# A decoder layer in one software pipeline: new instruction orders on all five engines, cross-attention turns issued singly, one-element VectorE copies removed

## The reference, cut to what matters

```python
x = x + attn(layernorm(x))              # 16 heads of 8, rope, causal
x = x + xattn(layernorm(x), ctx)        # 16 heads of 8, 77 context rows
x = x + ffn(layernorm(x))

def ffn(x):
    probs = softmax(x @ router_w)                     # 8 experts
    top1_val, top1_idx = top_1(probs)
    hid = (x @ up_w[e]) * silu(x @ gate_w[e])         # 7 routed experts
    routed = sum over e of (hid @ down_w[e]) * (top1_idx == e)
    shared = ((x @ shared_up) * silu(x @ shared_gate)) @ shared_down
    return 2.0 * top1_val * routed + shared
```

## Time and profile before

| | |
|---|---|
| median of 3 runs | 1080.29 us (1079.55 to 1080.8) |
| profiled execution, its own time | 1076.56 us |
| its span | 1074.7 us |
| TensorE busy, matmuls | 987.1 us (92%) |
| TensorE busy, weight loads | 819.5 us (76%) |
| VectorE busy | 870.5 us (81%) |
| ScalarE busy | 738.3 us (69%) |
| GpSimd busy | 631.6 us (59%) |

### The profile page before, as it was taken

One profiled execution on the slowest core, in us unless ns is written; L12 is line 12 of the kernel. 1 busy time (PEld: TensorE's weight loads), 2 busy tenths in 40 slices (PEclk: granted clock), 3 DMA queues, 4 the chain that ended last, 5 costly groups with the idle time before them and its releaser, 6 DMA issues.

```text
span 1074.7 us, 45099 instructions
## 1 busy us (share of the span) xinstructions
PE 987.1 (92%) x16200; PEld 819.5 (76%) x16201; DVE 870.5 (81%) x2853; ACT 738.3 (69%) x1557; POOL 631.6 (59%) x1488
## 2 busy tenths in 40 slices
PE   1578999999999999999999999999999889999995
PEld 1356777777777777777777777777777889999995
DVE  3367999989999999989999999999996557777774
ACT  0266887888888787888878888887875245555552
POOL 0345667776767767676677767677664224444443
PEclk9999999999999999999999999999999999999998
DMA  5222111000010000000000000100010122222220
GB/s 132 70 71 71 33 29 32 28 28 27 25 32 26 30 25 28 29 25 30 25 29 28 25 30 25 31 26 30 26 28 24 60 66 71 72 68 71 67 67 5
DMA packets 66648, 44.27 MB, mean 41 GB/s; under 512 B 24135, under 2 KB 61451, under 8 KB 66592
## 3 DMA queue, kind: packets, MB, share of 16 engines
q1 hardware_dynamic: 55424, 30.35, 10.5%
q0 software_dynamic: 5312, 12.18, 3.3%
q10 hardware_dynamic: 5856, 0.99, 0.5%
HBM read 23.96 MB, written 18.29 MB: 39 GB/s over the span
## 4 chain that ended last, share of the span: by engine, by line
PE 62%; SPq 16%; DMA 6%; DVE 6%; issue 5%; ACT 2%; ACTq 1%; POOL 1%; DVEq 0%; POOLq 0%
SPq L391 12%; PE pv L1120 9%; PE scores L1300 6%; PE scores L1305 6%; PE ro L1316 6%; DMA arena<-arena 5%; PE scores L999 5%; PE ro L1175 4%; PE scores L1161 3%; PE ro L1137 3%; PE st L1230 3%; DVE arena L641 3%; PE scores L1167 2%; PE ro L1148 2%; PE pj L1143 2%
## 5 line engine op out<-in xcount | busy, mean ns | idle before, releaser
L641 DVE TENSOR_REDUCE arena<-scores 128x8 f16<-128x1024 f32 (+1 forms) x256 | 256.6, 1002 | 61.3 <-PE scores L1007 50.9
L919 ACT ACTIVATE arena<-scores 128x1024 f32<-128x1024 f32 (+1 forms) x256 | 262.6, 1026 | 57.7 <-PE scores L1016 44.6
L859 ACT ACTIVATE arena<-st 128x128 f16<-128x128 f16 (+2 forms) x256 | 155.0, 606 | 6.4 <-PE st L1230 5.4
L859 ACT ACTIVATE arena<-arena 128x512 f16<-128x512 f32 (+2 forms) x192 | 92.9, 484 | 71.4 <-POOL arena L453 51.4
L1120 PE MATMUL pv<-arena 128*32 128x128 f32 (+1 forms) x4096 | 139.1, 277 | 0.1
L1120 PEld LDWEIGHTS pv<-arena 128*32 128x32 f32 (+1 forms) x4096 | 104.6, 110 | 17.2 <-issue 10.1
L439 POOL TENSOR_TENSOR arena<-arena,neg_half 128x1 f32<-128x1 f32 x192 | 106.5, 555 | 15.0
L449 POOL TENSOR_TENSOR arena<-arena 128x256 f32<-128x256 f32 x64 | 46.5, 726 | 81.5 <-DVE arena L633 81.5
L526 POOL DMA_INDIRECT out_dram<-x_tile x70 | 69.9, 998 | 38.6 <-POOL carried L525 26.1
L477 POOL TENSOR_TENSOR arena<-arena 128x128 f32<-128x128 f32 x128 | 51.8, 404 | 60.2 <-DVE arena L651 60.2
L814 DVE SCALAR_TENSOR_TENSOR half_hid<-tanh_s,scores 128x512 f32<-128x512 f32 x70 | 48.1, 688 | 40.7 <-ACT tanh_s L964 40.6
(11 more groups left out here) (175 smaller groups left out, 2696.5 us busy)
## 6 DMA issues: line engine op xcount, KB each, us to landing
x_tile<-xs SPq DMA_DIRECT2D x70, 129.0 KB, 2.1
arena<-arena SPq DMA_DIRECT2D x512, 4.0 KB
arena<-in_x_dram SPq DMA_DIRECT2D x64, 64.0 KB, 1.8
out_dram<-pay SPq DMA_DIRECT2D x64, 64.0 KB, 1.6
arena<-in_ctx_dram SPq DMA_DIRECT2D x64, 38.5 KB
w_gate<-in_L_ffn_gate_w_dram SPq DMA_DIRECT2D x7, 256.0 KB, 2.6
w_up<-in_L_ffn_up_w_dram SPq DMA_DIRECT2D x7, 256.0 KB, 3.0
w_down<-in_L_ffn_down_w_dram SPq DMA_DIRECT2D x7, 256.0 KB, 4.1
```

The costliest lines, as they stand in the source:

```text
L641: v.tensor_reduce(nmax[:, n, :].rearrange("p (m r s) -> p r m s", r=2, s=SLOT)[:, u, :, 0:HG], pair(s)[:, :, 0:HG * keys].rearrange("p m ( ...
L859: return a.activation(to, of, ACT.Copy)
L919: a.activation(e32[0:rows, 2 * n + u, :], scores[0:rows, 1024 * s:1024 * (s + 1)], ACT.Exp).then_inc(sexp_done[n][u], 1)
```

## The change

All five `step` tables are written anew, with other lags. On TensorE they run from 6 to 13, before from 2 to 8. `LAG` goes from 11 to 14. The self turns are still issued in pairs of mates, the four cross turns alone. `carry` and its four copies a step go; the waits that stood with them become pieces of their own (`stats_seen`, `resid_seen`) or fall away. Some waits are dropped or moved: `load_ctx` no longer waits for `ctxT_psum`, `values` waits for one exponential instead of two, `project_q2` no longer waits for `xT_ready`, `values_in` now waits for `rot_ready` and `xn3_out` for the scatter that last used its place.

```diff
-LAG = 11
+LAG = 14
...
             def load_ctx(b, p):
-                wait(sync, ctxT_psum, b - 1)
...
-            def carry(n):
-
-                v.tensor_copy(carried[:, n:n + 1], eps[:, :])
-
             def ln_stats_of(b, p, n):
...
-                    wait(dve, resid_done[0], b + 1)
                     rows = x1[:, p, :]
                 else:
-                    wait(dve, resid_done[1], b + 1)
                     rows = resid[:, b, :]
-                if n == 2:
-                    carry(3)
                 v.bn_stats(bn6[:, n, :], rows).then_inc(ln_stats[n], 1)
 
+            def stats_seen(b, p, n):
+
+                wait(dve, ln_stats[n], b + 1)
+
+            def resid_seen(b, p):
+
+                wait(dve, resid_done[1], b + 1)
+
             def ln_mean_var(b, p, n):
 
-                wait(dve, ln_stats[n], b + 1)
-                carry(n)
                 v.bn_aggr(mv[:, n, p, :], bn6[:, n, :]).then_inc(ln_mv[n], 1)
...
             def values_in(b, p):
+                wait(act, rot_ready, b + 1)
...
             def xn3_out(b, p):
                 wait(act, ln3_shift, b + 1)
+                wait(act, scattered[place(b, p)], sent(b, p))
...
             def values(b, p, n, *users):
                 vals, rows = ((val, P), (val2, C))[n]
-                wait(pe, sexp_done[n][0], b + 1)
                 wait(pe, sexp_done[n][1], b + 1)
...
             def project_q2(b, p, *users):
-                wait(pe, xT_ready[1], b + 1)
...
-                two_turns(i, p, cross_exp, 6, 1, 0, (((sh_hid, -1),), ((smax_done[0][0], 4),), ((sexp_done[0][0], 3),), ((smax_done[1][1], 1),), ((sexp_done[1][1], 0),),),
-                          cross_max, 5, 0, 1, (((sexp_done[0][1], 2),), ((smax_done[0][1], 3),), ((sexp_done[1][0], -1),), ((smax_done[1][0], 0),),))
...
+                at(i, p, 9, stacks2)
+                at(i, p, 10, cross_for_exp, 1, 0, ((sexp_done[0][1], 3),), ((smax_done[0][1], 4),), ((sh_hid, -2),), ((sexp_done[1][1], 0),))
```

More of the change, by code:

```diff
@@ L1284, in step @@
[L1284 to L1285 removed]
+                at(i, p, 9, values, 0, ((o_turned[1], -2),), ((o_turned[0], 0),))
```

196 lines of the change are left out of this document (99 added, 97 removed).

## The result

The changed kernel takes **1088.66 us** (median of 4 runs, 1086.64 to 1089.91), the kernel before on the same chip 1079.92: ratio 1.0091, 95% interval 1.007 to 1.0111. I had forecast 1079, a change of -1 us where +9 was measured. The measured time is above the forecast's own 1073 to 1085 and inside the whole range of 1062 to 1100. The profiled execution took 1088.46 us, span 1086.6; that of before 1076.56, span 1074.7.

A forecast was written before the change was run, and what follows sets the result against it. Bound: a loop through TensorE, ScalarE, SyncE's queue and a DMA landing. Copies 0, loop -2, fill -2, tail +3 sum to -1 us on the profiled 1076.56; with the median 3.7 above, 1079 us, likeliest 1073 to 1085, whole range 1062 to 1100.

The forecast's parts named there:

- What bounds the kernel before: Old pace, 12.11 us a step, set by a loop through TensorE, ScalarE, SyncE's queue and a DMA landing.
- The 1.1 us a step: TensorE's waits in the old step: add_attention 0.50, row-maximum DMAs 0.37, a turned-back tile 0.23.
- The trip: Row maxima through the DMAs: 4.47 us; with 3.8 of TensorE work meanwhile, some 0.6 us wait before the cross exp turn.
- The part from the cross exp turn to the next nmT_of 1: TensorE's work there summed to 7.68, taken as 7.6 us; plus 4.47 gives 12.07 us a step.
- Single cross turns: Four lone cross turns on TensorE in place of two pairs: 0.50 us a step more, 28 us over 56 steps.
- The copies: Removing VectorE's four one-element copies a step: costed at nothing; moved waits nothing, at worst 0.1 us.
- If the rows were not waited for: TensorE would need 7.6 + 3.8 = 11.4 us a step, time near 1042; chance 0.01.
- Fill and tail: Before and after the steady loop: fill -2 us (-6 to +6), tail +3 us (0 to +8).
- The bare pitches: Rival: TensorE's segment runs at bare pitches, 11.8 us a step, 1064 us; chance a quarter.
- The rival on entering and leaving row tiles: Each tiling change on TensorE costs: three more at 0.08 to 0.1, 12.3 us a step, 1090 us; chance 0.12.
- The rival with a late hand-off: Hand-off from self values through GpSimd's scaling to xT_of 1 comes late: 0.3 us, step 12.37, 1094 us; chance 0.15.
- The upper bound of the loop: Six entries at 0.08 and a late hand-off of 0.3 give 12.5 us a step, +22 us.

The follow-up runs named there:

- b2: Kernel before with only SyncE's order changed (self-maxima rows, context, input, cross-maxima rows, output): 1068.85 us, ratio 0.9896.
- a5: Changed kernel with TensorE's list beginning at cross_for_max 0 and values 0 alone moved ahead of the first cross exp turn: 1075.23 us, ratio 0.9963.
- a1: Changed kernel, same order of TensorE's work, but its list of a step begins at cross_for_max 0 instead of values 0: 1084.71 us, ratio 1.0049.
- a3: Changed kernel with the four one-element copies a step put back on VectorE: 1099.04 us, ratio 1.0187.
- b7: Kernel before with both mixed cross pairs issued as single turns, the second pair's kept apart by the transpose of the context: 1087.16 us, ratio 1.007.
- b1: Kernel before with its two mixed pairs of cross turns issued as four single turns in the same order: 1077.89 us, ratio 0.9989.
- b3: Kernel before without VectorE's four one-element copies a step, their waits moved to the next existing operations: 1084.73 us, ratio 1.0037.
- b4: Kernel before without VectorE's one-element copies and with SyncE's order changed: 1075.25 us, ratio 0.9959.
- a6: Changed kernel, list beginning at cross_for_max 0, second cross exp turn directly behind the first, ahead of values 0: 1095.45 us, ratio 1.0153.
- a2: Changed kernel with values 0 and the router's turn moved ahead of the first cross exp turn on TensorE: 1094.80 us, ratio 1.0137.
- a7: Changed kernel, list beginning at cross_for_max 0, values 0 ahead of the cross exp turn, transpose of x ahead of shared_gate: 1174.84 us, ratio 1.088.
- a9: Changed kernel, list beginning at cross_for_max 0, exp turns adjacent, router ahead of values, project_kv2 behind nmT_of 1: 1137.08 us, ratio 1.0544.
- b5: Kernel before, both cross pairs issued as single turns, kept apart by project_out 0 and ctxT_of: 1145.22 us, ratio 1.0617.

## Why the prediction was wrong, point by point

**What bounds the kernel before.** Half right. SyncE's queue was in the pace (b2), but its 0.37 us a step of wait was worth 0.11: VectorE's add_attention, 0.50 in the earlier trace rows, stood next and I had not made it the bound. The 1.1 us a step were waits of the weight loader, which runs ahead, and not all of them is time that the matmuls lost. For those the list of the kernel before has one wait:
```profile
PE scores L999 <- DMA arena<-arena: 6.6, 20, 0.4
```

**The trip.** Right: 4.47 forecast, 4.43 and 4.51 measured, and the wait is at the cross exp turn, once a step, 0.4 us at the loader (15.8 in 40); the self turns do not wait. a5 shows that it set the pace. The wait itself is 0.3 us, not 0.6: TensorE's work under the trip is 4.15 (a5) and not 3.8, most likely because I had taken the loader's 1.1 us off the old step as if TensorE had stood still for all of them. This did not change the pace, which is the trip and the part.

**The part from the cross exp turn to the next nmT_of 1.** This is the step that failed. I summed 7.68 and *took 7.6*; it measured 7.71 in one step and 7.95 in the next, mean 7.83. With 4.47 that is 12.30, which is the measured step. Of the 0.23 that were missing, 0.12 is the close of the hardware loop, 0.23 every second step (a1). It had stood in the kernel before where TensorE had work queued, and I had not asked about it when the list began somewhere else. Another 0.08 is what I took off for project_out, a guess towards the smaller number: the two are 0.30 and 0.32 instead of 0.33 twice, 0.04 less together, and other items are longer by more. The last 0.03 is the sum of the single items, 7.71 against 7.68, and that these agree is luck. By the start-to-start distances, in which the forecast was made, the router is 0.31 or 0.32 instead of 0.14, and the gate 0.99 instead of 0.95; the transpose of x 0.16 instead of 0.12 and project_kv2 0.50 instead of 0.47; against that shared_up and shared_down are 0.89 instead of 0.95, and the transpose of the maxima, positions and both projections a little shorter. The two exp turns and the two max turns are as forecast. With the copies put back the same part is 7.86 (a3), so the gain that I had left out also lies in it. The step came to 12.27 instead of 12.07, over 56 steps the 10.5 us between -2 and +8.5.

**Single cross turns.** Right in size: 0.35 twice and 0.25 twice, as forecast, the 0.23 of the loop's close apart; b7 shows 0.26 and 0.09 for one turn apart. b1 shows that the cost depends on the neighbour, not on the pair.

**The copies.** Wrong. I costed them at nothing because VectorE was idle 1.05 us a step. In the changed kernel their absence is worth 10 us (a3), without which it would stand near 1099. And the waits an operation ahead were not free either: "at worst 0.1 us" was the true price, and in the kernel before it stood in front of a result that TensorE waits for, 5 to 6 us (b3, b4).

**If the rows were not waited for, 11.4 us a step and 1042.** Wrong: a5 is that case nearly, with 12.01 and 1075. The 11.4 rests on the same 3.8; with 4.15 and 7.71 TensorE's own work is 11.86. Waits at several hand-offs are not slack that adds up; most of them only move.

**Fill and tail.** -1.1 and +5.2 against -2 and +3: right in sign, the tail 2 us short.

**Rivals.** The bare pitches did not come: the part is longer than the sum. The rival on entering and leaving row tiles came nearest in time, 12.3 us a step and 1090, but in good part by luck: of the 0.23 us that were missing, 0.12 is the loop's close. Its price per entry was right (0.09 in b7), and the rows show a trace of it in the part: the router takes 0.32 where a single turn stands behind it and 0.25 in a6, where a transpose does. How much of the pace such entries make was not measured. The rival with a late hand-off (1094) had a hand-off in the part, but what came was the loop's close and not GpSimd's scaling.

**Sums that do not come out.** The upper bound of the loop adds six entries at 0.08 and a hand-off of 0.3 to 12.07, which gives 12.85 and not 12.5. For the tail, 7 steps less 3.7 against 6 steps and 6.2 are 1.9 us and not 1.7. Neither moves the forecast.

## What to carry to other kernels

Where a pace is a wait plus the work behind it, everything in that work counts in full, the close of a hardware loop too: let the loop close where the engine has work queued, not behind the instruction that waits. Turns in different row tiles overlap when they are neighbours, paired or not; what costs is full-height work between them. When an item is moved in one engine's order, look in the other engines' fixed orders for who fills, reads or frees what it touches, and price that too: here three such edits paid (SyncE's queue, the loop's close, the values under the trip), and most others gave back what they saved or lost more.

## What the runs showed of the hardware that I had not expected

- The close of the two-step hardware loop costs TensorE 0.23 us directly behind a turn that was waited for (a1); behind shared_gate (a1), or between two cross turns ahead of which nothing was waited for (a2), nothing that the rows show.
- Two single turns in different row tiles, issued one after the other, take 0.38 or 0.39 us from the first start to the next item's (a2, b1), a mixed pair 0.35, and a kernel with them is as fast (b1); the time goes only when full-height work stands between (0.35 more for one, b7).
- A one-element copy moves VectorE's following operations by 0.07 us, while its row shows 0.15; a wait for the engine's own operation just ahead opens 0.1 us that the next one would have overlapped (a3, b3).
- A wait of 1.2 us in each step came with a mean granted clock of 0.96 instead of 0.986 (a7), and in the profiled execution about every fourth step ran at a mean of 0.88; a9 and b5, slower than the others too, kept 0.98 or more.
